# A norm's weights on VectorE instead of GpSimd, ahead of the maxima of a four-layer kernel's third layer

## The chip, the cores and the metric

The kernel runs on one core of a Trainium2 chip. The metric is the device time of one execution in microseconds (us), the median over several runs. A profiled execution comes with it: the hardware profiler's record of every instruction on every engine. The engines are TensorE (PE in the profile), VectorE (DVE), ScalarE (ACT), GpSimd (POOL) and SyncE (SP, which issues DMAs here). Each works through its own queue in order, and they meet at semaphores.

## What is computed

The reference is a stack of four layers over `x` of shape (4, 256, 256), which is 1024 tokens of 256 features. Each layer computes a gating of x (a scan over time, called the gain here) and a feed-forward part, and adds the result to x. The change lies in the third layer, a ternary-weight block with an RMS norm and 8-bit rounding of its activations:

```python
def activation_quant(x, num_bits=8):
    s = qp / jnp.clip(jnp.max(jnp.abs(xf), axis=-1, keepdims=True), EPS, None)
    return (jnp.clip(jnp.round(xf * s), qn, qp) / s).astype(x.dtype)

def rms_norm(x, weight, eps=RMS_EPS):
    var = jnp.mean(xf * xf, axis=-1, keepdims=True)
    return weight * (xf * jax.lax.rsqrt(var + eps)).astype(x.dtype)

h = jax.nn.silu(bit_linear(x, w_gate)) * bit_linear(x, w_up)
h = rms_norm(h, ln_weight)
return bit_linear(h, w_down)
```

`h` has 1024 features. The last `bit_linear` rounds the normed `h`, for which it needs the largest absolute value of each token's row.

## The kernel before

The code is written per engine, with every wait spelled out: `v` is VectorE, `act` ScalarE, `pool` GpSimd, `pe` TensorE, `sp` SyncE. The order on an engine is the order of the calls. In the third layer (`layer2`) the 1024 tokens are cut into eight tiles of 128 tokens, each a 128x1024 float32 slab `H[:, t]`. Tiles 0 to 5 (`EARLY2` = 6) are made first; tiles 6 and 7 are made between the roundings of the first ones.

For each tile TensorE makes gate and up products in two halves of 512 columns (`gates`, L1661), each half as soon as VectorE has read the banks of the same half of the tile before. ScalarE applies silu (L1490), VectorE multiplies silu and up into `H` (`hidden`, L1579, two instructions), and ScalarE squares the tile and sums each row (`squares`, L1497, semaphore `sq`), which is for the norm. The weights `LNW` are multiplied in place into `H[:, t]` by GpSimd once `sq` says that the squares of this tile have been taken (L1473, semaphore `lnd`). VectorE then takes the row maxima of the absolute values (`maxima`, L1573). After six tiles `factors(0)` combines the root of the summed squares with the maxima into the scales (L1586 to L1596, small). `rounds(u)` scales and rounds `H[:, u]` (L1600) and writes it as bf16 `HQ` (L1604); TensorE turns `HQ` (L1677), ScalarE copies the turned tile out (L1510), TensorE multiplies it by the down weights (L1688), the result is scaled into `OT` and turned back (L1696). After the turn back of tile 3 VectorE can add the first residual of the fourth layer (L2419).

VectorE's order in this layer is: hidden(0), hidden(1), hidden(2), maxima(0), hidden(3), maxima(1), hidden(4), maxima(2), hidden(5), maxima(3), maxima(4), one piece of the gain for later (four 512-column additions, L262 to L272), maxima(5), factors(0), rounds(0), hidden(6), rounds(1), hidden(7), out(0), rounds(2), maxima(6), out(1), rounds(3), maxima(7), factors(1). Tiles 4 to 7 are rounded in `layer3`, which first adds the residual. Behind its multiplications GpSimd goes on in `layer3` with a mask that waits for the fourth layer's `XC`.

Of the kernel before, what the change touches and what calls it, by code (L numbers as in the profile page):

```python
# [16 lines left out]
ALU = mybir.AluOpType  # L17
# [1377 lines left out]
def layer2(nc, k, io):  # L1395
# [3 lines left out]
    NT = T // P  # L1399
    done, k.numbers = k.numbers, []  # L1400
    with ExitStack() as ctx:
        def sb(name, shape, dt):
            return ctx.enter_context(nc.sbuf_tensor(name, shape, dt))
# [7 lines left out]
        LNW = sb("LNW2", [P, FF2], F32)  # L1411
# [10 lines left out]
        H = sb("H2", [P, NT, FF2], F32)  # L1422
# [43 lines left out]
        def gpsimd(pool):  # L1466
            pool.memset(EPS[:], 1e-6).then_inc(made, 1)

            pool.wait_ge(ln_in, 16)
            for t in range(NT):  # L1470

                pool.wait_ge(sq, t + 1)
                pool.tensor_tensor(H[:, t], H[:, t], LNW[:], ALU.mult).then_inc(lnd, 1)  # L1473

        def scalar(act):
            cond_scalar(act, k, cond)
# [64 lines left out]
        def vector(v):  # L1541
# [3 lines left out]
            for n in range(2):  # L1545
# [13 lines left out]
                for i in range(HALF2):  # L1559
                    t = n * HALF2 + i  # L1560
# [8 lines left out]

            def maxima(t):  # L1570

                v.wait_ge(lnd, t + 1)
                v.tensor_reduce(mx[:, t:t + 1], H[:, t], AX.X, ALU.max, apply_absolute_value=True).then_inc(hmx, 1)  # L1573

# [36 lines left out]
            for t in range(EARLY2):  # L1611
                hidden(t)
                if t >= 2:
                    maxima(t - 2)
            maxima(EARLY2 - 2)
            gain_pieces_done(v, k, rest[0:1])
            maxima(EARLY2 - 1)
            factors(0)
            for u in range(LATE2):
# [11 lines left out]
        def tensor(pe):  # L1631
# [89 lines left out]
            return turn_hidden, product, back  # L1721

        return sync, gpsimd, scalar, vector, tensor


# [1141 lines left out]
```

## Time and profile before

| | us |
|---|---|
| time, median of three runs | 874.04 (873.56 to 875.86) |
| the profiled execution, time | 873.79 |
| the profiled execution, span | 872.1 |
| TensorE busy | 752.6 (86%) |
| VectorE busy | 562.7 (65%) |
| ScalarE busy | 437.2 (50%) |
| GpSimd busy | 246.8 (28%) |
| TensorE's mean granted clock, as a share of 2.4 GHz | 0.947 |

The span is the time from the first to the last instruction in the trace. Busy times are sums over an engine's instructions. In views that are in order of time, a line gives the start, the time from there to the end of the last instruction that it merges, the engine, the line of the code, the operation, output and inputs, and the count; in brackets stands how long the engine had stood before it and who released it.

### The profile page before, as it was taken

What the parts mean: (1) busy time and instruction counts of PE and PEld (TensorE: products, weight loads), DVE (VectorE), ACT (ScalarE), POOL (GpSimd) and SP (SyncE); (2) the same over time, 40 slices, a digit from 0 to 9 for tenths busy, and PEclk for the clock granted to TensorE, in tenths of its full rate; (3) what the DMA queues carried; (4) which work ended last, traced back from release to release, by engine and by line L of the source; (5) the groups of instructions that cost most, each with busy time, mean ns of one, the idle gap of its engine ahead of it and who ended that gap; (6) DMA issues with size and microseconds to landing.
All of it is one profiled execution on the core that took longest, in us unless ns stands there. A gap on an engine that the chain in (4) does not pass through costs nothing.

```text
span 872.1 us, 11279 instructions
## 1 busy us (share of the span) xinstructions
PE 752.6 (86%) x3628; PEld 572.2 (66%) x3633; DVE 562.7 (65%) x1278; ACT 437.2 (50%) x878; POOL 246.8 (28%) x253
## 2 busy tenths in 40 slices
PE   0986686977875458899999999999998999999997
PEld 0433453634443137788888888888876788888885
DVE  5998899898797878656666666656664243223323
ACT  5895453234514756655555555645655243334342
POOL 5310112341250620202111111200123355555453
PEclk9999898789985977999999999999999999999999
DMA  4000002923222000210010110101011523314321
GB/s 154 2 2 1 0 0 85 413 76 104 90 69 77 1 0 1 98 49 22 28 50 1 48 51 1 37 1 38 1 50 39 157 61 86 88 32 85 85 56 48
DMA packets 37422, 49.84 MB, mean 57 GB/s; under 512 B 18574, under 2 KB 29942, under 8 KB 35702
## 3 DMA queue, kind: packets, MB, share of 16 engines
q1 hardware_dynamic: 36310, 46.90, 17.3%
q0 software_dynamic: 768, 2.10, 0.7%
q8 instruction: 30, 0.49, 0.2%
q10 hardware_dynamic: 288, 0.14, 0.1%
q14 instruction: 26, 0.21, 0.1%
HBM read 42.99 MB, written 6.13 MB: 56 GB/s over the span
## 4 chain that ended last, share of the span: by engine, by line
PE 58%; DVE 7%; ACT 3%; issue 1%; POOL 1%; DVEq 0%; ACTq 0%; POOLq 0%
PE bank L2048 15%; PE bank L2625 9%; PE bank L2064 8%; PE bank L2640 5%; PE bank L2620 5%; PE bank L2699 3%; PE bank L2716 3%; PE bank L2706 2%; PE bank L2698 1%; PE bank L2717 1%; PE bank L1661 1%; PE bank L1764 1%; PE bank L1688 1%; DVE PN L2522 1%; DVE mx L1573 1%
## 5 line engine op out<-in xcount | busy, mean ns | idle before, releaser
L2092 DVE TENSOR_TENSOR B_l<-bank,TW_l 128x512 f32<-128x512 f32 (+1 forms) x50 | 34.5, 690 | 134.9 <-PE bank L2048 134.9
L2259 POOL TENSOR_TENSOR WL<-RAW,WH 128x512 fp32r<-128x512 f32 x28 | 35.9, 1285 | 220.6 <-ACT WH L2292 220.6
L2117 POOL TENSOR_TENSOR HL_l<-H_l,HH_l 128x512 fp32r<-128x512 f32 (+1 forms) x50 | 64.9, 1298 | 112.5 <-ACT HH_l L2109 112.5
L2351 ACT ACTIVATE EX<-EX,nm 128x128 f32<-128x128 f32 (+1 forms) x128 | 57.0, 446 | 67.2 <-DVE nm L2513 67.2
L2101 ACT ACTIVATE S_l<-bank 128x512 f32<-128x512 f32 (+1 forms) x50 | 29.9, 598 | 86.8 <-PE bank L2048 86.7
L2527 DVE TENSOR_TENSOR AL<-bank,AH 128x256 fp32r<-128x256 f32 x64 | 26.9, 423 | 53.9 <-ACT AH L2365 53.9
L2625 PE MATMUL bank<-XH,WH 128*128 128x512 f32 x128 | 58.6, 458 | 0.7 <-DVE XL L1813 0.7
L2048 PE MATMUL bank<-XH,WH 128*128 128x512 f32 (+1 forms) x136 | 54.7, 402 | 0.0
L2048 PE MATMUL bank<-XH,WL 128*128 128x512 f32 (+1 forms) x136 | 54.1, 398 | 0.0
L2048 PE MATMUL bank<-XL,WH 128*128 128x512 f32 (+1 forms) x136 | 54.1, 398 | 0.0
L2109 ACT ACTIVATE HH_l<-H_l 128x512 fp32r<-128x512 f32 (+1 forms) x50 | 31.6, 633 | 38.0 <-PE bank L2064 30.5
L2625 PE MATMUL bank<-XH,WL 128*128 128x512 f32 x128 | 50.5, 395 | 0.0
L2625 PE MATMUL bank<-XL,WH 128*128 128x512 f32 x128 | 50.3, 393 | 0.0
L2509 DVE CUSTOM_DVE_ANT_0 EX<-bank,MASK 128x128 f32<-128x128 f32 (+1 forms) x128 | 40.7, 355 | 12.8 <-PE bank L2699 12.6
L2031 POOL TENSOR_TENSOR WL<-RAW,WH 128x512 fp32r<-128x512 f32 x27 | 35.3, 1307 | 47.5 <-ACT WH L2024 47.5
L161 POOL TENSOR_TENSOR WV<-EUK,V 128x512 f32<-128x512 f32 x16 | 22.7, 1424 | 85.4 <-DVE EUK L636 34.7
L552 ACT ACTIVATE MARK<-SC,THR 128x1536 bf16<-128x1536 bf16 (+1 forms) x30 | 43.0, 1509 | 5.1 <-PE bank L773 5.1
L2620 PE MATMUL bank<-WH,XH 128*128 128x256 f32 x128 | 38.7, 302 | 1.8 <-DVE K L2413 1.8
L2522 DVE TENSOR_SCALAR PN<-EX,rr 128x128 f32<-128x128 f32 (+1 forms) x128 | 38.4, 342 | 2.5 <-PE bank L2706 0.2
L2716 PE MATMUL bank<-PT,V 128*128 128x256 f32 x128 | 38.2, 380 | 1.7 <-DVE AL L2527 1.5
L2699 PE MATMUL bank<-K,Q 128*128 128x256 f32 x128 | 38.2, 380 | 0.0
L2365 ACT ACTIVATE AH<-bank 128x256 fp32r<-128x256 f32 x64 | 24.5, 384 | 25.9 <-PE bank L2717 24.4
(324 smaller groups left out, 2191.0 us busy)
## 6 DMA issues: line engine op xcount, KB each, us to landing
RAW<-l_attn SPq DMA_DIRECT2D x8, 1024.0 KB, 4.7
WE<-l_experts SPq DMA_DIRECT2D x1, 6144.0 KB, 23.3
TW_l<-routed SPq DMA_DIRECT2D x14, 256.0 KB, 4.2
RAW<-l_w SPq DMA_DIRECT2D x3, 1024.0 KB, 5.1
RAW<-l_experts SPq DMA_DIRECT2D x6, 512.0 KB, 3.9
TW_l<-routed SPq DMA_DIRECT2D x14, 192.0 KB, 3.3
sorted_x<-ZERO SPq DMA_DIRECT2D x1, 1920.0 KB, 8.1
XIN<-sorted_x SPq DMA_DIRECT2D x15, 128.0 KB, 2.1
```

The source lines that it names most:

```text
L552: act.activation(MARK[:, n % RING, 0:cols], SC[:, at:at + cols], ACT.Sign, bias=THR[:, i:i + 1]).then_inc(mark, 1)
L2048: mm = pe.matmul(self.k.banks[2 * (q % 2) + o][0:rows], w[i % self.SLOTS][:, at:at + rows], x[:, h, n * W:(n + 1) * W], start=(s == 0), st ...
L2064: mm = pe.matmul(self.k.banks[4 + 2 * m + n][:], w[i % self.SLOTS][0:rows, at:at + P], x[0:rows, q % 4], start=((i, f, s) == (0, 0, 0)), s ...
L2117: pool.tensor_tensor(self.HL[0:rows, q % 4], self.H[0:rows, q % 2], self.HH[0:rows, q % 4].bitcast(F32), ALU.subtract).then_inc(self.h_low, 1)
L2351: act.activation(EX[:, s, a:b], EX[:, s, a:b], ACT.Exp, bias=nm[:, s, i:i + 1], scale=scale, accum_out=rs[:, s, i:i + 1]).then_inc(expd, 1)
L2509: v.tensor_tensor_reduce(EX[:, s, a:b], banks[2 + s][:, a:b], MASK[:, 2 * P - (b - a):], 1.0, NEG, ALU.add, ALU.max, accum_out=mx[:, s, i: ...
L2522: v.tensor_scalar(PN[:, s, a:b], EX[:, s, a:b], rr[:, s, i:i + 1], None, ALU.mult).then_inc(normed, 1)
L2620: mm = pe.matmul(out[:, a * 2 * HD:(a + 1) * 2 * HD], x[:, h, t * P:(t + 1) * P], w[slot][:, at:at + 2 * HD], start=(p == 0), stop=(p == l ...
L2625: mm = pe.matmul(out[:], w[slot][:, at:at + HD], x[:, h, half * W:(half + 1) * W], start=(p == 0), stop=(p == len(passes) - 1))
L2640: mm = pe.matmul(bank[:], w[g % 2][:, at:at + P], x[:, head, here(i)], start=(head == 0 and p == 0), stop=(head == 1 and p == 2))
L2699: pe.matmul(out[:, P:3 * P], Q[:, n // 2, c + P:c + SEQ], K[:, n // 2, c:c + SEQ], start=True, stop=True).then_inc(scores, 1)
L2716: pe.matmul(out[:, 0:SEQ], V[:, t, d], PT[:, s, 0:SEQ], start=True, stop=False)
```

## The change

GpSimd loses its eight multiplications by `LNW`, and VectorE gets them, as the first thing in `maxima(t)`. The semaphores keep their meaning: VectorE waits for the weights' DMA and for the tile's squares, multiplies in place, counts `lnd` up, and waits for `lnd` ahead of the maximum, so that the reduction reads finished data. Nothing else changes.

```diff
@@ -1466,11 +1466,6 @@
         def gpsimd(pool):
             pool.memset(EPS[:], 1e-6).then_inc(made, 1)
 
-            pool.wait_ge(ln_in, 16)
-            for t in range(NT):
-
-                pool.wait_ge(sq, t + 1)
-                pool.tensor_tensor(H[:, t], H[:, t], LNW[:], ALU.mult).then_inc(lnd, 1)
 
         def scalar(act):
             cond_scalar(act, k, cond)
@@ -1569,6 +1564,9 @@
 
             def maxima(t):
 
+                v.wait_ge(ln_in, 16)
+                v.wait_ge(sq, t + 1)
+                v.tensor_tensor(H[:, t], H[:, t], LNW[:], ALU.mult).then_inc(lnd, 1)
                 v.wait_ge(lnd, t + 1)
                 v.tensor_reduce(mx[:, t:t + 1], H[:, t], AX.X, ALU.max, apply_absolute_value=True).then_inc(hmx, 1)
 
```

## Rows read from the trace of the kernel before

**Rows 1.** Busy time by stretch: PE, PEld, DVE, ACT, POOL, then clock, DMA.

```profile
264.00:300.00 36.00, 20.09 (x86) 9.90 (x88) 29.62 (x54) 24.29 (x35) 13.67 (x7) 0.77 0.13 44
300.00:350.00 50.00, 31.02 (x201) 23.87 (x201) 39.25 (x67) 28.43 (x44) 7.22 (x5) 0.76 0.00 1
350.00:600.00 250.00, 247.78 (x1462) 218.18 (x1463) 158.61 (x575) 139.21 (x411) 36.93 (x29) 1.00 0.11 37
```

**Rows 2.** Lines L1473 and L1573: durations in ns, and who waited for GpSimd.

```profile
L1473 POOL TENSOR_TENSOR H<-H,LNW x8: 2344/2364/2815, 285.1 to 314.0; 128x1024 f32<-128x1024 f32 x8
...
  DVE mx L1573: 1.6, 2
...
L1573 DVE TENSOR_REDUCE mx<-H x8: 1205/1214/1222, 287.5 to 318.0; 128x1 f32<-128x1024 f32 x8
```

**Rows 3.** The chain of waits in the third layer: start, us, what.

```profile
285.09 2.37 POOL H L1473
...
295.89 2.36 POOL H L1473
```

**Rows 4.** VectorE in order of time, tiles 1 to 5.

```profile
283.07 1.61 DVE L1579 SCALAR_TENSOR_TENSOR H<-bank,KU,S 128x512 f32<-128x512 f32 x2 [1.19 <-ACT S L1490]
285.68 1.62 DVE L1579 SCALAR_TENSOR_TENSOR H<-bank,KU,S 128x512 f32<-128x512 f32 x2 [0.99 <-ACT S L1490]
287.48 1.22 DVE L1573 TENSOR_REDUCE mx<-H 128x1 f32<-128x1024 f32 x1 [0.19 <-POOL H L1473]
288.62 1.40 DVE L1579 SCALAR_TENSOR_TENSOR H<-bank,KU,S 128x512 f32<-128x512 f32 x2
...
298.27 1.22 DVE L1573 TENSOR_REDUCE mx<-H 128x1 f32<-128x1024 f32 x1 [1.42 <-POOL H L1473]
299.41 1.68 DVE L262 TENSOR_TENSOR DF<-DF,DB 128x512 f32<-128x512 f32 x1
301.01 0.68 DVE L264 TENSOR_TENSOR NF<-NF,NB 128x512 f32<-128x512 f32 x1
...
302.82 1.21 DVE L1573 TENSOR_REDUCE mx<-H 128x1 f32<-128x1024 f32 x1
```

**Rows 5.** Durations by line (ns) and VectorE's first rounding.

```profile
L1248 DVE TENSOR_TENSOR HT<-ST,bank x15: 391/414/423, 186.3 to 243.4; 128x256 f32<-128x256 f32 x15
...
L272 DVE TENSOR_TENSOR NF<-NF,WV x6: 677/680/683, 103.0 to 302.2; 128x512 f32<-128x512 f32 x6
...
305.13 0.75 DVE L1600 TENSOR_SCALAR H<-H,s 128x1024 f32<-128x1024 f32 x1
305.92 0.69 DVE L1604 TENSOR_SCALAR HQ<-H 128x1024 bf16<-128x1024 f32 x1
```

**Rows 6.** GpSimd in order of time, tiles 4 and 5, and tile 7.

```profile
295.89 4.65 POOL L1473 TENSOR_TENSOR H<-H,LNW 128x1024 f32<-128x1024 f32 x2 [0.29 <-ACT SQ L1497]
...
314.01 2.81 POOL L1473 TENSOR_TENSOR H<-H,LNW 128x1024 f32<-128x1024 f32 x1 [1.77 <-ACT SQ L1497]
```

**Rows 7.** TensorE in order of time, from the gates of tile 6.

```profile
294.75 1.90 PE L1661 MATMUL bank<-WT,QT 128*128 128x512 bf16 x8 [0.70 <-DVE H L1579]
306.67 1.04 PE L1677 MATMUL bank<-IDB,HQ 128*128 128x128 bf16 x8 [10.02 <-DVE HQ L1604]
307.50 3.62 PE L1661 MATMUL bank<-WT,QT 128*128 128x512 bf16 x8
```

**Rows 8.** VectorE and TensorE in order of time, the tail.

```profile
316.06 1.32 DVE L1600 TENSOR_SCALAR H<-H,s 128x1024 f32<-128x1024 f32 x1
...
318.16 0.86 PE L1677 MATMUL bank<-IDB,HQ 128*128 128x128 bf16 x8 [2.63 <-DVE HQ L1604]
...
324.36 1.29 DVE L2419 TENSOR_TENSOR X<-X,bank 128x512 f32<-128x512 f32 x2 [4.13 <-PE bank L1696]
```

**Rows 9.** ScalarE in order of time, the end of tile 5's squares.

```profile
296.87 0.19 ACT L1497 ACTIVATION_READ_ACCUMULATOR SQ<-H 128x1 f32 x1
```

**Rows 10.** Busy time by stretch, 4 us (columns as in rows 1).

```profile
300.00:304.00 4.00, 0.00 (x0) 0.00 (x0) 4.00 (x6) 1.29 (x3) 0.54 (x1) 0.67 0.00 0
```

## The prediction

> **What bounds the kernel now.** I read the page's busy shares first, which average over stages, then the kernel cut into stretches, then the line that moves, the chain of waits, and each engine of the third layer in order of time. From 350 to 600 us TensorE is busy 99% of the time; in the third layer (264 to 345 us) it is not, and VectorE and ScalarE carry the stage: 29.6 and 24.3 of 36 us up to 300, against 20.1 for TensorE [rows 1]. So what happens to VectorE here counts at full price unless it had been waiting, and whatever delay leaves the stage is carried to the end, because nothing later is idle enough to take it back: the fourth layer starts from this layer's residual.
>
> GpSimd's only work here is the eight multiplications of H by LNW, 2.36 us each. They ran behind other work: VectorE waited for them twice, 1.6 us in all [rows 2]. The chain of waits shows two places. In the first, tiles 0 to 5, the chain passes through two of GpSimd's multiplications, one at 285.09 and one at 295.89, and the maxima behind them [rows 3]. In the second, TensorE stands 2.63 us for HQ of tile 3 and turns it at 318.16; the products and turns up to the residual at 324.36 hang on it [rows 8]. In between TensorE stood 10.02 us for the first HQ [rows 7].
>
> **The price of one multiplication on VectorE.** No row shows a 128x1024 float32 product of two SBUF tensors there. A two-input instruction takes 0.414 us at 256 columns (one input in PSUM) and 0.680 at 512 [rows 5]; the step of 0.266 for 256 columns gives 0.680 + 2 x 0.266 = 1.21 at 1024, and the 1024-column reduction takes 1.21 [rows 2]. I take 1.22. The new reduction waits for the product just ahead of it. Such a wait on the engine's own result costs 0.04 us: L1600 starts at 305.13, lasts 0.75, and L1604 starts at 305.92 [rows 5]. So 1.26 us per tile. The lower bound is 2 x 0.60 = 1.20 (the additions of L264 to L272 follow each other by 0.60; three of them lie between 301.01 and the maximum at 302.82 [rows 4]), the upper bound 2 x 0.68 + 0.04 = 1.40. Below nothing is excluded: the instructions are added to a queue, and only relief elsewhere, counted apart, can pay for them.
>
> **Tiles 0 to 5.** The six multiplications add 6 x 1.26 = 7.56 us ahead of factors(0). What VectorE sheds: from 287.22 (0.08 before the end of tile 2's hidden(), the overlap between two instructions that do not wait) to 302.82, the start of the sixth maximum, 15.60 us pass. The work in it is five maxima at 1.14 start to start, three hidden() pairs at 2 x 0.67 and four 512-column additions at 0.60 [rows 4]: 5.70 + 4.02 + 2.40 = 12.12. The other 3.48 us are waits for GpSimd (0.19 and 1.42), waits for ScalarE's silu between pairs, and one stretched addition (L262, 1.68 instead of 0.68). I take all of it as shed, because VectorE will always be the late one. That needs two things. First, the silu must be ahead: after the first half of a tile's hidden() TensorE and ScalarE need no more than 2.6 us until the next tile's first half can start, which is the period of the early pairs, where VectorE waited for the silu (283.07 to 285.68 [rows 4]); the new period is 1.34 + 1.14 + 1.26 = 3.74. Second, sq must be ahead: the square of tile 5 ended at 297.06, and moves only with hidden(5), by some 3 us, while its multiplication starts at about 305.6 [rows 9]. So the shift at factors(0) is 7.56 - 3.48 = +4.1 us.
>
> **L262's stretch.** The addition at 299.41 took 1.68 us while a GpSimd product ran until 300.54; the one at 301.01, after it, took 0.68 [rows 4, 6]. The rounding at 316.06 took 1.32 us against 0.75 for the same form at 305.13, while GpSimd's last product ran 314.01 to 316.82 [rows 5, 6, 8]. The change leaves GpSimd without work in this layer, so I let both stretches go: 1.00 (already in the 3.48) and 0.57. The Trainium skill, "SBUF — State Buffer", on the shared port pair, says the pair is an exclusive lock that the first of the two engines keeps for its whole instruction. By that rule the addition, issued at 299.41, would have stood 1.13 us, until 300.54, so the relief would be 1.13 rather than 1.00, and the sum 0.1 us smaller.
>
> **Tiles 6 and 7.** maxima(6) stands ahead of rounds(3): its multiplication is the seventh on the path, +1.26, and rounds(3) gets 0.57 back. Its sq is early: the later square, of tile 7, had let GpSimd start by 314.01 in the old run [rows 6], and tile 6's product comes to about 318.6. The eighth, in maxima(7), and factors(1) lie behind HQ of tile 3. VectorE then stood 4.13 us until the residual [rows 8]; 1.26 fits, and if that cover were gone it would cost the full 1.26. Nobody reads the second factors ahead of rounds(6), behind that residual. Queued behind each new wait on VectorE are that tile's maximum and the next hidden(), for which TensorE's gates and ScalarE's silu wait. That is the whole effect, already counted.
>
> **GpSimd and the queues.** Removing its eight instructions leaves it free from the EPS memset on. Its next work, the mask, waits for the fourth layer's XC, so nothing starts sooner; no DMA goes through this part of its queue, and SyncE's next load waits for the EPS memset, which stays. Price: nothing.
>
> **Sum.** +4.1 + 1.26 - 0.57 = +4.8; with unrounded steps (7 x 1.26 = 8.82 less 3.48 and 0.57) 4.77. Start from the profiled execution: span 872.10, time 873.79, so 1.69 lie outside the span. 873.79 + 4.77 = 878.6. The profiled time is 0.25 below the median of 874.04; I forecast 878.6, which is +0.52% on the median.
>
> **TensorE's clock** is the part that the sum leaves out. In the old run it fell from 2.4 to 1.2 GHz at about 301 us, after TensorE had stood since the gates of 294.75, and a tile's eight gates products took 1.90 us before and 3.62 at 307.50 [rows 7, 10]. The new gap (the sixth gates end about 299.7, first HQ at about 310.7) is equally long, so the fall and the slow products come in both. But TensorE now works 1.9 of 3.74 us per early tile rather than 1.9 of 2.6. If the clock fell there too, a tile's second half would come 3.62 (both groups) + 0.7 (silu) + 0.7 (itself) after the end of the first half before it, less the 0.67 in which both overlap: about 4.35 us instead of 3.74, some 0.65 for each of three tiles, +2.0. And the clock may return earlier or later relative to the tail's products, which the trace cannot tell: I allow 1.2 us either way (several groups of eight products in the tail take about 2 us at 1.2 GHz and half at 2.4).
>
> **Rivals.**
>
> (a) The chain view taken at its word: only the two products it names matter. Against 2.37 + 2.36 us of GpSimd stand two of 1.26 on VectorE: -2.2 us, 871.6. It is one mechanism, in tiles 0 to 5, and decides if the other five multiplications find VectorE idle; that takes 6.3 us of idle time ahead of HQ(3), and rows 4 show 3.48 in all, waits included. Chance 0.02. The Trainium skill, "GPSIMD Engine Reference", section 4.1, advises VectorE for an elementwise product on a tile and calls GpSimd about twice slower; taken alone it speaks for this outcome. The trace agrees on the speed (2.36 [rows 2] against my 1.22), but not on whose time counts.
>
> (b) The product runs as fast as VectorE's one-input float32 rounding, 0.75 + 0.04 for 1024 columns [rows 5]: 7 x 0.79 - 4.05 = +1.5, 875.3, no measurable change. It decides below (2.6 + 4.05) / 7 = 0.95 us each, 4.05 being the 3.48 and 0.57 that are shed. Against: a two-input row of 512 columns already takes 0.68 [rows 5], and half of 0.79 is 0.40. Chance 0.03.
>
> (c) The tail hides part of the delay because HQ(3) is not what is late: under +2.6. Against: TensorE's 2.63 us of standing ends with it [rows 8]. Chance 0.03.
>
> (d) No relief: the two stretches have another cause and stay, 4.77 + 1.57 = +6.3, 880.1. Against: both coincide with a GpSimd product. Chance 0.05.
>
> (e) The clock falls in tiles 3 to 5 as well: +6.8, 880.6. Chance 0.07.
>
> (f) The change does not do what it says because VectorE stands for ScalarE's squares. The smallest lead is that of tile 0, whose square had let GpSimd start at 285.09 [rows 3] and whose product can start at 287.22; price 0. Chance under 0.01.
>
> **How the numbers follow.** The forecast, 878.6, gets 0.80. Its own span: 7 x 1.20 and a favourable clock give 873.79 + 8.40 - 4.05 - 1.2 = 876.9; 7 x 1.40 with no clock effect gives 879.5, an unfavourable clock 880.7. With (d) and (e) inside, the range is 876.8 to 880.8, which leaves out (a), (b), (c) and little else. A measurement of this kernel can tell about 0.3% (2.6 us) from no change, so slower means above 876.7: 0.80 + 0.05 + 0.07, and 0.02 for mishaps, 0.94. The same: 0.045, for (b), most of (c). Faster: 0.015, most of (a).
>
> **What would show it.** Eight DVE products at about 1.22 us; maxima no longer waiting for GpSimd; L262 at 0.68 and every L1600 near 0.75; rounds(0) near 309.2 instead of 305.13, HQ(3) ending near 322.9, the residual near 329.1, and the fourth layer unchanged but for that shift. I am wrong if a product takes under 0.95 us, if L262 stays at 1.68, if VectorE waits for silu between tiles 3 and 5 (the clock), or if the shift at the residual differs by over 1 us from that at HQ(3).

## The result

The changed kernel takes 878.11 us in the median of ten runs (876.35 to 880.93), the kernel before 873.90 in the same session. The ratio is 1.0039 with a 95% interval of 1.0028 to 1.0049: slower by 4.2 us in the medians, 3.4 by the ratio, 2.4 to 4.3 by its interval. The forecast was 878.6, +4.77 us.

The profiled execution of the changed kernel took 878.28 us, with a span of 876.6. VectorE in order of time, tiles 0 to 5 of the third layer, answers to [rows 4]:

```profile
281.31 1.41 DVE L1577 SCALAR_TENSOR_TENSOR H<-bank,KU,S 128x512 f32<-128x512 f32 x2 [1.42 <-ACT S L1485]
...
288.05 1.22 DVE L1569 TENSOR_TENSOR H<-H,LNW 128x1024 f32<-128x1024 f32 x1
289.30 1.22 DVE L1571 TENSOR_REDUCE mx<-H 128x1 f32<-128x1024 f32 x1
290.43 1.40 DVE L1577 SCALAR_TENSOR_TENSOR H<-bank,KU,S 128x512 f32<-128x512 f32 x2
...
297.83 0.74 DVE L1577 SCALAR_TENSOR_TENSOR H<-bank,KU,S 128x512 f32<-128x512 f32 x1
299.29 0.75 DVE L1577 SCALAR_TENSOR_TENSOR H<-bank,KU,S 128x512 f32<-128x512 f32 x1 [0.71 <-ACT S L1485]
...
304.72 0.68 DVE L262 TENSOR_TENSOR DF<-DF,DB 128x512 f32<-128x512 f32 x1
...
310.70 0.75 DVE L1598 TENSOR_SCALAR H<-H,s 128x1024 f32<-128x1024 f32 x1
```

The product takes 1.22 us, the maximum follows 1.25 us after its start, and no maximum waits for anyone. L262, 1.68 us in [rows 4], takes 0.68. From tile 2's hidden() at 286.51 to the first rounding at 310.70 VectorE works without a break but for one wait of 0.71 us for ScalarE's silu, at 299.29. The tail answers to [rows 8]:

```profile
322.50 0.74 DVE L1598 TENSOR_SCALAR H<-H,s 128x1024 f32<-128x1024 f32 x1
323.28 0.69 DVE L1602 TENSOR_SCALAR HQ<-H 128x1024 bf16<-128x1024 f32 x1
...
324.03 1.03 PE L1675 MATMUL bank<-IDB,HQ 128*128 128x128 bf16 x8 [3.32 <-DVE HQ L1602]
324.86 1.92 PE L1686 MATMUL bank<-WT,HT 128*128 128x256 bf16 x8
326.57 0.63 PE L1694 MATMUL bank<-IDF,OT 128*128 128x128 f32 x2
328.25 1.89 PE L1686 MATMUL bank<-WT,HT 128*128 128x256 bf16 x8 [1.05 <-ACT HT L1505]
```

The rounding of tile 3 is back to 0.74 us from 1.32. TensorE now stands 3.32 us for its HQ instead of 2.63. Both groups of down products shown (L1686, tiles 2 and 3) take 1.9 us.

The two executions did not reach the third layer at the same moment, so I count from the start of the layer's first hidden(): 280.47 before, 281.31 after. The last column is the time from the residual to the end of the span. The lines e1 to e12 are experiments, described below; the numbers in brackets are against before. There is one trace of each kernel.

| us after the first hidden() | first rounding | HQ(3) ends | residual (L2419) | residual to end |
|---|---|---|---|---|
| before | 24.66 | 37.63 | 43.89 | 547.74 |
| after | 29.39 (+4.73) | 42.66 (+5.03) | 50.19 (+6.30) | 545.10 |
| predicted | +4.1 | +4.8 | +4.8 | |
| e1, no product | 21.69 (-2.97) | 34.02 (-3.61) | 40.91 (-2.98) | 547.51 |
| e2, tiles 0 to 5 | 29.39 (+4.73) | 41.96 (+4.33) | 48.40 (+4.51) | 547.28 |
| e3, tiles 6 and 7 | 24.67 (+0.01) | 38.09 (+0.46) | 45.62 (+1.73) | 548.93 |
| e4, after, products twice | 36.15 (+11.49) | 50.51 (+12.88) | 58.04 (+14.15) | 547.35 |
| e5, after, GpSimd busy | 33.17 (+8.51) | 47.74 (+10.11) | 54.18 (+10.29) | 547.57 |
| e6, after, TensorE awake early | 28.59 (+3.93) | 42.15 (+4.52) | 48.59 (+4.70) | 547.20 |
| e7, after, TensorE awake | 28.63 (+3.97) | 41.79 (+4.16) | 46.99 (+3.10) | 545.06 |
| e8, before, TensorE awake | 24.67 (+0.01) | 37.17 (-0.46) | 42.37 (-1.52) | 544.93 |
| e9, before, additions moved | 22.42 (-2.24) | 37.23 (-0.40) | 44.69 (+0.80) | 548.91 |
| e10, after, additions moved | 26.19 (+1.53) | 40.36 (+2.73) | 46.69 (+2.80) | 547.64 |
| e11, e9 and tile 7 | 22.43 (-2.23) | 34.44 (-3.19) | 40.60 (-3.29) | 547.66 |
| e12, e11, TensorE awake | 22.45 (-2.21) | 33.41 (-4.22) | 39.26 (-4.63) | 544.65 |

The part of the excess that the queue does not explain (4.73 for 4.1, and 6.30 for 4.8) is TensorE's clock, by the rows that follow and by e6 below. The changed kernel by stretches (PE, PEld, DVE, ACT, POOL, then clock, DMA):

```profile
288.00:292.00 4.00, 1.90 (x10) 0.66 (x9) 3.97 (x6) 2.79 (x6) 0.00 (x0) 1.00 0.01 2
292.00:296.00 4.00, 2.97 (x8) 0.90 (x8) 3.97 (x5) 2.41 (x4) 0.00 (x0) 0.54 0.02 4
296.00:300.00 4.00, 3.62 (x9) 0.98 (x8) 3.26 (x5) 2.12 (x3) 0.00 (x0) 0.61 0.00 0
...
324.00:328.00 4.00, 3.17 (x18) 2.33 (x18) 3.20 (x8) 1.19 (x2) 0.00 (x0) 0.50 0.00 0
```

The clock fell to 1.2 GHz at about 292.3 and returned at about 299, where the kernel before held 2.4 GHz all through the early tiles. Ahead of the fall TensorE had worked 1.90 of 4 us. In the tail it was low again from about 323, and both groups of down products, those of tiles 2 and 3, took 1.9 us. In the kernel before only the first did: the second took 1.05, the clock having come back ahead of it.

The last column varies by up to 4.3 us, as much as the change costs, and most of that arises far behind the third layer. From the residual to the instruction of L2485 that starts at 665.15 us in the kernel before, all fourteen kernels need 340.8 to 342.1 us. From there to the end, where their code is the same, four need 202.9 to 203.1 us (after, e7, e8, e12), three 206.9 to 207.0 (before, e3, e9) and the others 205.9 to 206.1. It goes with the clock again. In those four the granted clock is 1.00 from 660 to 680 and from 680 to 700 us, and 0.99 from 850 us on. In the others one or both of the first two stretches have 0.83 to 0.92, and the last has 0.81 to 0.94. The same stand of TensorE can end either way. TensorE before, then after:

```profile
674.63 0.77 PE L2064 MATMUL bank<-HH_l,WH 128*128 128x512 f32 x1 [3.53 <-POOL HL_l L2117]
675.19 0.63 PE L2064 MATMUL bank<-HL_l,WH 128*128 128x512 f32 x1
```

```profile
683.09 0.47 PE L2062 MATMUL bank<-HH_l,WH 128*128 128x512 f32 x1 [3.53 <-POOL HL_l L2115]
683.39 0.39 PE L2062 MATMUL bank<-HL_l,WH 128*128 128x512 f32 x1
```

So the profiled pair was 7.14 us apart at the residual (0.84 of it from ahead of the layer) and 8.45 by 368 us. It was 5.90 apart from 706 us on, the clock of the kernel before having fallen at 673, and 4.49 at the end, where it had fallen at 864 once more.

### The profile page after: what moved, and what is told of

It reads as the page before. It is cut to its first block, busy times and chain, and to the rows that moved or that the text cites. A ratio compares the mean times of both kernels' runs of the same rounds, so it can differ in the third digit from the quotient of the medians.

```text
span 876.6 us, 11286 instructions
## 1 busy us (share of the span) xinstructions
PE 756.8 (86%) x3628; PEld 573.2 (65%) x3633; DVE 571.0 (65%) x1286; ACT 437.6 (50%) x878; POOL 226.8 (26%) x245
## 4 chain that ended last, share of the span: by engine, by line
PE 57%; DVE 8%; ACT 2%; issue 2%; POOL 0%; DVEq 0%; ACTq 0%
PE bank L2046 15%; PE bank L2623 9%; PE bank L2062 8%; PE bank L2638 5%; PE bank L2618 5%; PE bank L2697 3%; PE bank L2714 3%; PE bank L2704 2%; PE bank L2696 1%; PE bank L2715 1%; PE bank L1659 1%; DVE H L1569 1%; PE bank L1762 1%; DVE PN L2520 1%; DVE mx L1571 1%
```

## The experiments

Each was measured beside the kernel before, in the same session; ratios are to that. The 4 us at stake are small against the spread of a single run, so the marks of the table above carry the argument about the layer; the medians, which take in the last column too, say what a kernel costs.

**e1: no product at all.** The diff against the changed kernel:

```diff
-                v.wait_ge(ln_in, 16)
                 v.wait_ge(sq, t + 1)
-                v.tensor_tensor(H[:, t], H[:, t], LNW[:], ALU.mult).then_inc(lnd, 1)
-                v.wait_ge(lnd, t + 1)
```

> The multiplication by the norm's weights is left out on both engines; the maxima wait for the squares only. Theory A (the change puts eight products into VectorE's queue, of which seven count, and takes away what GpSimd's products cost): against before the time falls by the waits and stretches that GpSimd causes and by nothing else, since the early tiles go back to their period of 2.6 us with its waits for silu: 0.19 + 1.42 + 1.00 + 0.57 = 3.2 us, so about 870.7. VectorE has no wait for GpSimd and no addition or rounding above 0.8 us in this layer. Rival 'no relief' (rival d of the prediction: the two stretches have another cause): only the waits go, 1.6 us, 872.3, and the addition L262 stays at 1.68 us.

Measured: 870.70 us against 874.26, ratio 0.9952 (0.9933 to 0.9971). VectorE:

```profile
295.79 2.34 DVE L1568 TENSOR_REDUCE mx<-H 128x1 f32<-128x1024 f32 x2
298.05 0.68 DVE L262 TENSOR_TENSOR DF<-DF,DB 128x512 f32<-128x512 f32 x1
```

The two maxima (tiles 3 and 4) follow each other, and the addition takes 0.68 us. Theory A's number holds, and "no relief" falls: the stretch went with GpSimd's product. So what GpSimd's products had cost the kernel before, waits and stretches together, is 3.0 us at the residual and 3.6 in the medians (2.5 to 5.9 by the interval). The change exchanges that for 7 x 1.25 = 8.75.

**e2 and e3: the two halves of the change.** `ON_V` is (0, 1, 2, 3, 4, 5) in e2 and (6, 7) in e3; GpSimd keeps the others. The main part of the edit:

```diff
-                v.wait_ge(lnd, t + 1)
+                if t in ON_V:
+                    v.wait_ge(ln_in, 16)
+                    v.wait_ge(sq, t + 1)
+                    v.tensor_tensor(H[:, t], H[:, t], LNW[:], ALU.mult).then_inc(lnv, 1)
+                    v.wait_ge(lnv, sum(i <= t for i in ON_V))
+                else:
+                    v.wait_ge(lnd, sum(i not in ON_V for i in range(t + 1)))
```

> Only tiles 0 to 5 are multiplied on VectorE, tiles 6 and 7 stay on GpSimd. Theory A: +7.56 - 3.48 = +4.1 us on before, 878.0, so nearly all of the change's cost; the rounding of tile 3 may stay stretched by GpSimd's last product (1.3 us instead of 0.75). Rival 'the tail': if the cost lay in tiles 6 and 7 and in TensorE's clock in the tail, this kernel would stand within 1 us of before, 874.9 at most.

Measured: 877.97 against 874.26, ratio 1.0045 (1.0032 to 1.0058), as theory A had it. The rounding of tile 3 stayed stretched, and its lines show why: VectorE first, GpSimd second.

```profile
320.22 1.33 DVE L1607 TENSOR_SCALAR H<-H,s 128x1024 f32<-128x1024 f32 x1
```

```profile
318.26 2.74 POOL L1474 TENSOR_TENSOR H<-H,LNW 128x1024 f32<-128x1024 f32 x1 [1.38 <-ACT SQ L1498]
```

GpSimd's product ends at 321.00, the rounding at 321.55: 0.55 us behind it.

> Only tiles 6 and 7 are multiplied on VectorE, tiles 0 to 5 stay on GpSimd. Theory A: +1.26 - 0.57 = +0.7 us on before, 874.6; the product of tile 7 is hidden behind the products of tiles 2 and 3 on TensorE. With e2 it adds up to the whole change: 4.1 + 0.7 = 4.8. Rival: if the product of tile 7 is not hidden, +2.0, 875.9.

Measured: 876.03 against 874.26, ratio 1.0012 (1.0000 to 1.0024), that is 0 to 2.1 us; 0.7 lies inside, but the median says 1.8. The trace tells the two apart. HQ(3) ends 0.46 us later than before, close to the 0.7 expected, and tile 7's product starts behind it and ends long before the residual, so it is hidden. Yet the residual comes 1.73 later. TensorE in the tail of e3:

```profile
319.00 1.03 PE L1684 MATMUL bank<-IDB,HQ 128*128 128x128 bf16 x8 [3.32 <-DVE HQ L1611]
319.83 1.92 PE L1695 MATMUL bank<-WT,HT 128*128 128x256 bf16 x8
...
323.23 1.89 PE L1695 MATMUL bank<-WT,HT 128*128 128x256 bf16 x8 [1.05 <-ACT HT L1511]
```

Both products ran at 1.2 GHz, as in the changed kernel; before, the second took 1.05. The seventh product lengthens TensorE's standing ahead of HQ(3) from 2.63 to 3.32 us, and it is tempting to blame that. But e6 (below) has the same 3.3 us, and there the second of the two products ran at 2.4 GHz again: 6.44 us from HQ(3) to the residual, against 7.53 here and in the changed kernel, and 6.26 before. And e1 and e9, which have no VectorE product in the tail and stand 2.06 us there, have the slow second product too. So the slow tail is not a fixed part of the change. The two halves add up to 5.7 thousandths against 3.9 for the whole; with intervals of 1.8 and 1.1 on these they agree only just.

**e4: every product twice.** The first product is followed by a second one that waits for it.

> As the changed kernel, but VectorE multiplies each tile twice (so the output has the weights squared); the second product waits for the first. Theory A: seven more products of 1.26 us on the path, +8.8 us on the changed kernel, less the silu waits that the changed kernel still has (0.7 us in its profiled run): 878.1 + 8.1 to 8.8 = 886.2 to 886.9. Tile 7's second product makes 2.5 us behind the standing time of 4.1 us and still costs nothing. Rival 'clock': if TensorE's falls to 1.2 GHz made up a good part of the cost, more standing of TensorE would add several us beyond that, to 889 or more.

Measured: 887.35 against 874.26, ratio 1.0160 (1.0144 to 1.0177). The gap of 13.1 us less the change's own 4.2 is 8.9 for seven more products, 1.27 each; by the ratios it is 10.6 (8.9 to 12.3), 1.5 each, so the times alone give the price only roughly. The first rounding comes 36.15 us after the first hidden(), 6.76 behind the changed kernel's; 6 x 1.25 less the 0.71 of silu wait is 6.79. That confirms the price per product without a look at its duration. The residual is 7.85 later than the changed kernel's, where 8.1 to 8.8 were expected, so a further cost from the clock did not appear in the layer.

**e5: GpSimd busy for nobody.**

```diff
+            pool.wait_ge(ln_in, 16)
+            pool.wait_ge(qb, 2)
+            for t in range(NT):
+
+                pool.wait_ge(sq, t + 1)
+                pool.wait_ge(scr, t)
+                pool.tensor_tensor(Q32[:, 0], LNW[:], LNW[:], ALU.mult).then_inc(scr, 1)
```

> The changed kernel, but GpSimd makes its eight products all the same, at the old moments, from the weights into a tile that nobody reads. No one waits for them. Theory A (the relief comes from GpSimd being silent): VectorE's two-input instructions in SBUF and its roundings that meet a GpSimd product are stretched again, L262 or its neighbours above 1 us, and several of the new products of 1.21 us are stretched by up to 1.2 us; 878.1 + 2 to + 7, near 882. Rival 'no relief' (the two engines do not disturb each other): 878.1, all VectorE products at 1.21 us.

Measured: 884.82 against 875.03, ratio 1.0116 (1.0100 to 1.0132), some 6.7 us above the changed kernel by the ratios, 5.6 in the medians, and 3.99 at the residual. VectorE, then GpSimd:

```profile
295.26 2.57 DVE L1576 TENSOR_TENSOR H<-H,LNW 128x1024 f32<-128x1024 f32 x1
...
300.32 2.83 DVE L1576 TENSOR_TENSOR H<-H,LNW 128x1024 f32<-128x1024 f32 x1
```

```profile
294.86 1.90 POOL L1475 TENSOR_TENSOR Q<-LNW 128x1024 f32<-128x1024 f32 x1 [3.17 <-ACT SQ L1499]
```

GpSimd's product ran 294.86 to 296.76. VectorE's, issued at 295.26, ended at 297.83, 1.07 us after GpSimd's end and nearly its own length of 1.22. It did not run at half speed beside it, it stood until GpSimd was done. Ahead of the first rounding four products are stretched so, by 4.60 us in all; the rounding comes 3.78 later than in the changed kernel, whose silu wait of 0.71 is gone here. "No relief" is refuted from the other side. The Trainium skill, "SBUF — State Buffer", on the shared port pair, calls this an exclusive lock held for the whole instruction; these lines agree with it.

**e6 and e7: the clock held up in the changed kernel.** `keep` gives TensorE products into a bank that nobody reads; e6 has only the last line, e7 all with 38, 10 and 10.

```diff
+            def keep(n, bank):
+
+                for _ in range(n):
+                    pe.matmul(banks[bank][:], QT[:, 0, 0, 0:P], WT[:, 0, 0:W], start=True, stop=True)
+
...
+                if u == 0:
+                    keep(38, 7)
+                if u == 3:
+                    keep(10, 3)
+                if u == 4:
+                    keep(10, 3)
...
+                if t >= 2:
+                    keep(4, 7)
```

> The changed kernel, and TensorE makes four more products of 512 columns, into a bank that is free, after the gates of tiles 2 to 5 each. Theory A with the clock as a side term: in the changed kernel's profiled run the clock stood at 1.2 GHz from 292.6 to 299.1 and VectorE waited 0.7 us for silu in it. Awake, that wait goes: -0.7 us, 877.4. The step at which the first rounding starts is then 7.56 - 3.48 = 4.1 us later than before's, counted from the layer's start. Rival 'the clock does not matter there': 878.1. Rival 'the products are in the way': 878.6 or more.

Measured: 878.04 against 875.03, ratio 1.0032 (1.0018 to 1.0046). The ratio is 0.0007 below the changed kernel's, inside the noise, so the time does not decide. The trace does. The clock stayed at 2.4 GHz until about 306, and the silu wait is gone:

```profile
297.73 1.40 DVE L1577 SCALAR_TENSOR_TENSOR H<-bank,KU,S 128x512 f32<-128x512 f32 x2
...
309.80 0.75 DVE L1598 TENSOR_SCALAR H<-H,s 128x1024 f32<-128x1024 f32 x1
```

Counted from 281.21, the first rounding comes at 28.59, +3.93 on before, and the residual at +4.70. The sum by VectorE's queue had 4.1 and 4.8.

> As e6, and TensorE also fills its long gap ahead of the first rounded tile with 38 such products, and the gaps ahead of tile 3's and tile 4's turns with 10 each. The changed kernel's profiled run shows 1.2 GHz from 305 to 316 and from 323 to 346. Theory: gates of tile 7 in 1.9 us instead of 3.45 (-1.6 us), the products of tiles 2 and 3 in 1.05 instead of 1.9 each (-1.7 us), the silu wait (-0.7 us), so -4 us, 874.1. If the clock's falls are not on the path: 878.1.

Measured: 875.77 against 875.03, ratio 1.0015 (0.9998 to 1.0032). It is 2.1 us below the changed kernel by the ratios (3.5 in the medians), where 4 was expected. The residual came 3.2 us earlier than in the changed kernel's trace (46.99 for 50.19), but the gates of tile 7 were not saved:

```profile
300.65 8.37 PE L1667 MATMUL bank<-WT,QT 128*128 128x512 bf16 x37
311.72 0.62 PE L1686 MATMUL bank<-IDB,HQ 128*128 128x128 bf16 x8 [2.71 <-DVE HQ L1602]
312.38 2.83 PE L1659 MATMUL bank<-WT,QT 128*128 128x512 bf16 x8
```

The filling ended 2.71 us before HQ came, and the clock fell at about 313, in the gates.

**e8: the same in the kernel before**, with 34, 8 and 10 products and none in the early tiles.

> The kernel before, with the gap ahead of the first rounded tile filled with 34 products, and 8 and 10 ahead of tile 3's and tile 4's turns. Its profiled run shows 1.2 GHz from 301.5 to 311.5, from 318.3 to 321.7 and from 328.8 to 338.7. Theory: gates of tile 7 -1.7 us, the products of tile 2 -0.85 us, 871.3. e7 minus e8 is then the price of the change with the clock held up in both: 4.8 us if the queue alone decides, clearly less if the changed kernel's extra falls of the clock make up a part of the measured 4.2.

Measured: 873.46 against 875.03, ratio 0.9982 (0.9964 to 1.0000), 12 runs between 867.50 and 876.29, a far wider spread than before's. Its profiled run is one of the quick ones, and there the residual comes at 42.37, 1.5 us earlier than before's. e7 less e8 is 4.6 us at the residual, near the 4.8 of the queue, but 2.9 by the ratios, with intervals of 1.5 us on each. So this pair does not settle how much of the measured cost is the clock's. What makes e8's runs scatter was not shown, but the table has a candidate: in its profiled run the clock did not fall between 660 and 700 us, and the time behind the residual is 2.8 us shorter than before's.

**e9 and e10: four additions out of the way.** The gain piece (L262 to L272) goes from ahead of the sixth maximum to behind the second factors, where VectorE stands.

```diff
-            gain_pieces_done(v, k, rest[0:1])
             maxima(EARLY2 - 1)
...
             factors(1)
+            gain_pieces_done(v, k, rest[0:1])
```

> The kernel before, with the four additions of the gain (L262 to L272) moved from between the fifth and the sixth maximum to behind the second factors, where VectorE stands 4.13 us before the residual. Theory A: the sixth maximum then follows the fifth as soon as GpSimd's product of tile 5 is there (300.54 in the old run), so the first rounding comes at about 300.6 + 1.2 + 1.1 = 302.9 instead of 305.13: -2.2 us. The additions (2.5 us) fit into the standing time. 871.7 to 872.8, counted from the before of the same job. Rival 'the stage is set elsewhere': no change.

Measured: 872.25 against 874.59, ratio 0.9973 (0.9958 to 0.9989), -2.3 us. The sixth maximum now waits for GpSimd, and the first rounding comes 22.42 us after the first hidden() (278.90), 2.24 earlier than before:

```profile
296.70 1.22 DVE L1573 TENSOR_REDUCE mx<-H 128x1 f32<-128x1024 f32 x1 [1.42 <-POOL H L1473]
299.00 1.22 DVE L1573 TENSOR_REDUCE mx<-H 128x1 f32<-128x1024 f32 x1 [1.08 <-POOL H L1473]
...
301.32 0.76 DVE L1600 TENSOR_SCALAR H<-H,s 128x1024 f32<-128x1024 f32 x1
```

Most of that gain is gone at HQ(3), which ends only 0.40 us earlier, and the residual comes 0.80 later than before's. The moved queue met GpSimd's last product at another place. VectorE's rounding of tile 2, which takes 0.69 us elsewhere, then GpSimd:

```profile
310.45 2.77 DVE L1604 TENSOR_SCALAR HQ<-H 128x1024 bf16<-128x1024 f32 x1
```

```profile
310.34 2.34 POOL L1473 TENSOR_TENSOR H<-H,LNW 128x1024 f32<-128x1024 f32 x1 [1.91 <-ACT SQ L1497]
```

The rounding started 0.11 us behind GpSimd's product and ended 0.54 us behind its end, stretched by 2.08 us. This execution took 874.24 us, near the top of e9's runs (870.17 to 874.79), so the median gain is not to be read off this trace; how often the two meet was not measured.

> The changed kernel with the same four additions moved behind the second factors. Theory A (VectorE's queue alone decides): they leave the path with 4 x 0.60 = 2.4 us; behind them the standing time has held the eighth product (1.26) as well, 4.13 us in the changed kernel's profile after it, so they still fit: -2.4 us on the changed kernel, about +1.8 us on the before of the same job. That is 4.0 us above e9, less than the 4.8 between the two kernels only by the relief of L262 that e9 doesn't need.

Measured: 877.52 against 874.59, ratio 1.0029 (1.0014 to 1.0044), 2.5 us by the ratio where 1.8 was expected; e10 less e9 is 5.3 in the medians, 4.9 by the ratios (1.9 either way), where 4.0 was. The first rounding is at 26.19, 3.20 earlier than in the changed kernel: the 2.4 of the additions, and the silu wait of 0.71, which this execution did not have. So the step is as theory A has it; the whole came out 0.7 above, with an interval of 1.3 either way.

**e11 and e12: what the parts add up to.** e11 is e9 with `ON_V` = (7,); e12 is e11 with `keep` of 26, 8 and 10.

> As e9, and the product of tile 7 alone is on VectorE, where it lies behind the last rounding that TensorE waits for; the other seven stay on GpSimd. Theory A: the rounding of tile 3 loses its stretch (1.32 us to 0.75) and the product costs nothing: -0.6 us on e9, so about -2.8 us on before. Rival: the product is not hidden, +0.7 on e9.

Measured: 871.71 against 874.59, ratio 0.9966 (0.9953 to 0.9978), -2.9 us, as expected. The rounding of tile 3 takes 0.74 us, and so does e9's; what e11's trace has over e9's is that no rounding meets a product, which is 2.08 of the 2.79 us between them at HQ(3). The product costs nothing, but its cover is nearly used up: VectorE stands 0.22 us ahead of the residual, for 4.13 before. In the times e11 and e9 lie 0.6 us apart, which is not clear of noise.

> As e11, and TensorE fills the gap ahead of the first rounded tile with 26 products, and the gaps ahead of tile 3's and tile 4's turns with 8 and 10, as in e8. If the clock's falls cost what e8's profiled run shows (the residual 1.5 us earlier, counted from the layer's start, than before's): -1.5 us on e11, -4.3 us on before. If e8's median gain of 1.6 us holds with its wide spread: between -3 and -5. Rival: the filled gaps only move the fall of the clock to another place, then as e11 with a wider spread.

Measured: 867.84 against 874.59, ratio 0.9925 (0.9901 to 0.9950), six runs. That is 6.6 us below before and beats both kernels; it is more than the 4.3 expected of it, and past the range of 3 to 5. The traces of e11 and e12 are 3.1 us apart, and only 1.34 of it lies between the first hidden() and the residual, near the 1.5 expected. Another 3.01 lies behind the residual, all of it behind 660 us, where e11's clock fell and e12's did not, and 1.25 the other way ahead of the layer. Why the filling should reach that far is not shown; the changed kernel has no filling, and its trace is as short there. In the layer e12's stretches show what the filling did here and not in e7 and e8:

```profile
304.00:308.00 4.00, 1.72 (x14) 0.76 (x13) 3.79 (x12) 0.66 (x1) 0.00 (x0) 1.00 0.00 0
308.00:312.00 4.00, 2.78 (x22) 1.61 (x22) 3.29 (x6) 4.00 (x7) 2.36 (x1) 1.00 0.01 2
```

The clock held 2.4 GHz from 283 to 326, and the gates of tile 7 ran at it:

```profile
306.68 0.62 PE L1695 MATMUL bank<-IDB,HQ 128*128 128x128 bf16 x8 [2.19 <-DVE HQ L1611]
307.34 1.90 PE L1668 MATMUL bank<-WT,QT 128*128 128x512 bf16 x7
```

TensorE stood 2.19 us behind the filling here, 2.71 in e7 and 2.68 in e8. Whether that half microsecond made the difference was not tested.

## Why the prediction was right, point by point

Where the layer is concerned, the sum held: +5.03 at the end of HQ(3) for +4.8. That the whole kernel's time came out within 0.5 us of the forecast is in part luck. The prediction let a delay that leaves the layer be carried to the end, because nothing later is idle enough to take it back. No idle time took it back, but the clock did: the profiled pair went from 8.45 us apart to 4.49, because the kernel before lost its clock twice behind 660 us and the changed one hardly. The cost by the ratio, 3.4 us (up to 4.3), lies below the 4.77 of the queue as well.

**The price of a product.** 1.22 us and 1.25 per tile stood against 1.22 and 1.26; e4's first rounding gives 1.25 from the marks alone ((6.76 + 0.71) / 6). Taking the two-input rows of 256 and 512 columns and going on in a line was good to a hundredth. Rival (b) falls.

**What VectorE sheds.** 3.48 us were predicted for tiles 0 to 5. With the clock up (e6) the shift at the first rounding is 3.93, so 7.50 - 3.93 = 3.57 were shed. e1 shows 2.97 without the new queue, when part of the silu waits remains. The relief of 0.57 in the tail came in the changed kernel, in e3 and in e11, and failed to come in e2, which left GpSimd its product there. Rival (d) falls. The relief of L262 was 1.00, not the 1.13 that the lock's rule gave: the stretched addition ended 0.55 us behind GpSimd's product, not its full 0.68.

**The eighth product is hidden**, shown by e3, where VectorE still stands 4.14 us ahead of the residual, and by e11, where 0.22 is left.

**The chain view** (rival a, 871.6) was wrong by its sign: two products on the chain did not mean that only two count. The queue behind them was full.

**The clock** was the step that the prediction left open, and there two of its own signs of error came up. VectorE did wait for silu between tiles 3 and 5, and the residual shifted by 1.27 us more than HQ(3). In the profiled execution the mechanism of rival (e) took place, though I had given it 0.07. Its price was mis-sized: 0.7 us, not 2.0, since the clock fell during the gates of tile 4 and returned during those of tile 6, and VectorE's longer queue covered the rest. The tail's 1.2 us either way was about right: 1.27 between HQ(3) and the residual (7.53 for 6.26), 1.09 of it gone in e6. In the ten runs these effects do not show as a sum: the median of +4.2 lies below even the queue's 4.8. The kernel before pays for falls of the clock elsewhere, as told above. The term is real in the traces, but its mean over runs is not established.

## What to carry to other kernels

An instruction moved to a faster engine costs its full length there unless that engine stands still: compare the added time with the idle time of the receiving queue ahead of the point that the next stage waits for, not with the duration on the engine it left. Here 8.8 us came in and 4.1 went out. The move costs nothing where it lies behind that point (tile 7); that it pays there is argued from the stretches that it removes, since e11's 0.6 us on e9 is not clear of noise. Looking for that point also shows which unrelated work stands ahead of it: four additions gave back 2.3 us in the medians by a change of place, and used up most of the standing time. And a queue that is moved meets the other engine's instructions elsewhere, as e9's rounding of tile 2 did.

Before a difference of a few us is put down to an edit, it is worth splitting it by a mark behind the edited stage. Here the part from 665 us on, where the code is the same, varied by 4 us.

## What the runs showed that I had not expected

A fall of the granted clock can be moved by a change that does not touch TensorE. The kernel before held 2.4 GHz through the early gates. With VectorE's longer queue behind them, the same gates lost it at 290 to 293 us in the changed kernel, e2, e4 and e5, and did not in e10; with four more products per tile (e6, e7) they kept it. And the filling of gaps gives uneven returns: in e7 and e8 the clock fell inside the gates that it was meant to speed up, or just ahead of them, while in e12 it held for 43 us. That was worth 1.34 us at the residual; the 3.6 us by the ratios (0.9966 to 0.9925), where 1.5 was expected, are mostly not from this layer in the traces. A stand of TensorE of 3.53 us, the same in both kernels, cost the one before its clock and the changed one nothing.
